# Attention and routed experts on one core: maxima, values and layer norms move from VectorE to ScalarE and GpSimd

## What is computed

```python
x = x + _layernorm(_L0_attn_ref(_layernorm(x), w_qkv, w_out, b_out))
x = x + _layernorm(_L0_ffn_ref(_layernorm(x), ...))
# _L0_ffn_ref:
for l in range(L):                                   # L = 2
    x = x + _attn(_ln(x, ln1_w[l], ln1_b[l]), wq[l], ..., bv[l], bo[l])
    h = _ln(x, ln2_w[l], ln2_b[l])
    moe = _token_moe if l % 2 == 0 else _seq_moe     # 2 of 8 experts, by token or by sequence
    x = x + moe(h, gate_w[l], gate_b[l], e_w1[l], e_b1[l], e_w2[l], e_b2[l])
# _attn: v = x @ wv + bv ; y = softmax(q k / sqrt(8), causal) @ v ; return y @ wo + bo
```

## Time and profile before

| | before |
|---|---|
| median of 3 runs | 1293.72 us (1292.19 to 1295.46) |
| the profiled execution | 1296.67 us |
| its span | 1295.0 us |
| TensorE busy | 1063.0 us (82%) |
| VectorE busy | 966.4 us (75%) |
| ScalarE busy | 711.1 us (55%) |
| GpSimd busy | 663.9 us (51%) |
| granted TensorE clock, mean | 0.957 |

### The profile page before, as it was taken

One profiled execution on the slowest core, in us unless ns is written; L12 is line 12 of the kernel. 1 busy time (PEld: TensorE's weight loads), 2 busy tenths in 40 slices (PEclk: granted clock), 3 DMA queues, 4 the chain that ended last, 5 costly groups with the idle time before them and its releaser, 6 DMA issues. The chain is left out here.

```text
span 1295.0 us, 36482 instructions
## 1 busy us (share of the span) xinstructions
PE 1063.0 (82%) x10163; PEld 786.2 (61%) x10258; DVE 966.4 (75%) x3059; ACT 711.1 (55%) x1502; POOL 663.9 (51%) x986
## 2 busy tenths in 40 slices
PE   1788888888899888888369999178788888868997
PEld 0565555556666565656269999145455555547996
DVE  3789999999989999899533333178888989855665
ACT  1466566666666656655145655145566566644564
POOL 3345555555555777776721111555666767422332
PEclk9999999999999999999679999589999999988999
DMA  5332111111111221121022222233312212100000
GB/s 148 99 92 68 50 49 34 41 49 51 52 45 40 63 65 49 54 62 43 33 87 70 72 69 70 66 104 101 86 42 64 63 40 62 51 2 5 20 19 22
DMA packets 120792, 74.56 MB, mean 58 GB/s; under 512 B 7936, under 2 KB 115712, under 8 KB 120704
## 3 DMA queue, kind: packets, MB, share of 16 engines
q1 hardware_dynamic: 101536, 54.48, 15.1%
q10 hardware_dynamic: 15072, 10.61, 2.9%
q0 software_dynamic: 4096, 8.40, 2.2%
HBM read 22.21 MB, written 12.71 MB: 27 GB/s over the span
## 5 line engine op out<-in xcount | busy, mean ns | idle before, releaser
L489 ACT ACTIVATE prob<-bank 128x512 f32<-128x512 f32 x576 | 341.5, 597 | 264.1 <-PE bank L319 151.5
L560 DVE TENSOR_REDUCE negm<-bank 128x2 f32<-128x512 f32 (+1 forms) x576 | 388.6, 678 | 53.0 <-PE bank L297 43.1
L861 POOL TENSOR_SCALAR_AFFINE_SELECT prob<-prob 128x512 f32<-128x512 f32 x384 | 248.7, 650 | 168.3 <-ACT prob L489 166.5
L338 PE MATMUL bank<-prob,vaug 128*32 128x256 f32 (+1 forms) x3072 | 165.9, 334 | 1.5 <-POOL prob L861 1.2
L305 PE MATMUL bank<-stack 126*128 126x256 bf16 x768 | 149.2, 275 | 0.0
L324 PE MATMUL bank<-stack 128*128 128x256 bf16 x768 | 147.8, 273 | 0.9 <-ACT prob L489 0.9
L1152 POOL COPY w_job<-w_s 128x512 f32 x72 | 47.1, 655 | 192.2 <-PE bank L1122 183.5
L1133 PEld LDWEIGHTS bank<-w_job,prob 128*128 128x128 f32 x1152 | 139.7, 192 | 3.6
L1133 PE MATMUL bank<-w_job,prob 128*128 128x128 f32 x1152 | 139.9, 275 | 0.0
L1144 ACT ACTIVATE prob<-bank,b_job 128x256 f32<-128x256 f32 x288 | 118.2, 469 | 16.1 <-PE bank L1122 14.6
L338 PEld LDWEIGHTS bank<-prob,vaug 128*32 128x32 f32 x3072 | 80.8, 109 | 75.7 <-issue 43.2
(11 more groups left out here) (174 smaller groups left out, 1971.6 us busy)
## 6 DMA issues: line engine op xcount, KB each, us to landing
stack<-parts SPq DMA_DIRECT2D x288, 128.0 KB
w_s<-e_w ACTq DMA_DIRECT2D x32, 256.0 KB, 2.9
oT<-x_routed SPq DMA_DIRECT2D x40, 128.0 KB, 2.1
y_routed<-oT SPq DMA_DIRECT2D x40, 128.0 KB, 1.8
stack<-mT SPq DMA_DIRECT2D x192, 4.0 KB
out<-x_all SPq DMA_DIRECT2D x16, 128.0 KB, 1.8
b_all<-e_b ACTq DMA_DIRECT2D x2, 512.0 KB, 8.3
x_routed<-hk,x_at POOLq DMA_INDIRECT x64, 2.3
```

What stands on the lines that cost most here:

```text
L338: m = nc.tensor.matmul(o, w, (prob0, prob1)[kb][:, g % 2, h], start=kb == 0, stop=kb == 1, skip_group_check=True)
L489: nc.scalar.activation(o, s, ACT.Exp, scale=SCALE).then_inc(exp_done, 1)
L560: nc.vector.tensor_reduce(o, s, AX.X, ALU.max, negate=True).then_inc(max_done, 1)
L861: nc.gpsimd.affine_select(out=t, in_=t, compare_op=ALU.is_ge, fill=0.0, base=0, pattern=[[0, HG], [1, P]], channel_multiplier=-1).then_inc ...
```

## The change

Eight things change, all of them in the attention pipelines:

- mT is copied by ScalarE (`act_mT`, after the slot's first exponential) instead of VectorE.
- v is copied to vaug by ScalarE without its bias (`act_values`, first in slot 3). The bias is folded into the output bias once at the start: since the softmax weights sum to one, bv @ wo is added to bo (`pe_fold_T`, `act_fold`, `pe_fold`, `dve_fold`).
- v's products go to slot 2 and to another bank (the upper half of `mid_bank`), behind a wait for mT; the waits on `v_sb` stand before transposes of maxima.
- xn is made by ScalarE (`act_xn`, slot 3, after mT) as Identity(r x + c), with c = -mean r made by GpSimd (`pool_shift`, two small operations after the root).
- hn likewise (`act_hn`, end of slot 2).
- f likewise (`act_f`, end of slot 1, where it was in slot 0 on VectorE).
- att of phase 0 is made by GpSimd (`pool_att`, last of its slot 2's own work); `dve_x` waits for it.
- Counters of the semaphores follow.

```diff
-        v_bank, lg_bank = post_bank[:, 0:T], post_bank[:, T:T + 2 * E]
+        v_bank, lg_bank = mid_bank[:, T:2 * T], post_bank[:, T:T + 2 * E]
         rank_bank, sum_bank = post_bank[:, T + 4 * E:T + 6 * E], post_bank[:, T + 6 * E:T + 7 * E]
+        fold_bank = [pv_bank[:, n * P:(n + 1) * P] for n in range(3)]
...
-            pe.wait_ge(res, NRES * i.v + NRES)
+            pe.wait_ge(hn_ok, 2 * (i.v - B) + 2)
...
-                if nxt:
-                    pe.wait_ge(v_sb, nxt.v + 1)
...
+                if gm == 0:
+                    pe.wait_ge(v_sb, im.v + 1)
+                if gm == 2 and nxt:
+                    pe.wait_ge(v_sb, nxt.v + 1)
                 pe_max_T(im, gm)
...
-            if k == 1 and nxt:
+            if k == 2 and nxt:
+                if im:
+                    pe.wait_ge(mT_sb, 4 * im.v + gm + 1)
                 pe_v(nxt)
...
+        def act_mT(i, g):
+            act.wait_ge(maxT_ps, 4 * i.v + g + 1)
+            need(act, row_dma[g % 2], rows_ready(i, g) - 16)
+            nc.scalar.copy(mT[:, g % 2], mid_bank[0:2 * HG, 0:P].bitcast(BF16)).then_inc(mT_sb, 1)
...
+        def act_values(i):
+
+            act.wait_ge(v_ps, i.v + 1)
+            need(act, pv_ps, 4 * (i.v - 2) + 4)
+            if isinstance(i.v, int) and i.v == 0:
+                act.wait_ge(kstack_ok, 2)
+            nc.scalar.copy(vaug[:, i.par].rearrange("p j h c -> p (j h) c")[:, :, 0:HD],
+                           v_bank.rearrange("p (s d) -> p s d", d=HD)).then_inc(v_sb, 1)
...
+        def pe_fold_T():
+
+            pe.wait_ge(later_ld, LATER)
+            for n in range(3):
+                m = nc.tensor.transpose(fold_bank[n], bv_s[:, n], ident[:])
+            m.then_inc(fold_ps, 1)
...
+        def pe_fold():
+            pe.wait_ge(fold_sb, 3)
+            for n in range(3):
+                m = nc.tensor.matmul(fold_bank[n], bvT[:, n], wo_s[:, n], start=True, stop=True)
+            m.then_inc(fold_ps, 1)
...
+        def dve_fold():
+            dve.wait_ge(fold_ps, 2)
+            for n in range(3):
+                nc.vector.tensor_tensor(bo_s[:, n], fold_bank[n], bo_s[:, n], ALU.add).then_inc(bo_ok, 1)
...
+        def act_normal(dst, src, r, c, s):
+
+            for j in range(2):
+                nc.scalar.activation(dst[j], src[j], ACT.Identity, scale=r[:, j:j + 1],
+                                     bias=c[:, j:j + 1]).then_inc(s, 1)
...
+        def act_xn(i):
+            act.wait_ge(pre_rstd, NPRSTD * i.v + NPRSTD)
...
+        def act_hn(i):
+            act.wait_ge(post_rstd, NRSTD * i.v + NRSTD)
+            need(act, hT_ps, i.v - B - 1)
+            if i.phase == 1:
+                need(act, hk_sb, i.v - B - 1)
+            act_normal([hn[:, i.par, j] for j in range(2)], tiles(f_all, i), post_r[:, i.par], post_c[:, i.par],
...
+        def act_f(i):
+            act.wait_ge(post_rstd, NRSTD * i.v + NRSTD)
+            act_normal(tiles(f_all, i), tiles(x_all, i), r2[:, i.par], c2[:, i.par], f_ok)
...
-            cur, nxt, nxt2, old, older = (item(step, d) for d in (0, 1, 2, -1, -2))
...
+            cur, nxt, nxt2, old, older, oldest = (item(step, d) for d in (0, 1, 2, -1, -2, -3))
...
+            if k == 3 and nxt:
+                act_values(nxt)
             if io:
                 act_oT(io, go)
             if ie:
                 act_exp(ie, ge, 0)
+            if im:
+                act_mT(im, gm)
+            if k == 3 and nxt2:
+                act_xn(nxt2)
...
+            if k == 1 and oldest and oldest.phase == 0:
+                act_f(oldest)
+            if k == 2 and older and older.phase > 0:
+                act_hn(older)
...
-        def dve_mT(i, g):
-            dve.wait_ge(maxT_ps, 4 * i.v + g + 1)
-            need(dve, row_dma[g % 2], rows_ready(i, g) - 16)
-            nc.vector.tensor_copy(mT[:, g % 2], mid_bank[0:2 * HG, 0:P].bitcast(BF16)).then_inc(mT_sb, 1)
...
+            need(dve, post_rstd, NRSTD * (i.v - 2) + 4)
+            dve_moments(post_st, post_mv[:, i.par], res, summed(i), 1 if i.phase == 0 else NRES - 5)
 
         def dve_x(i):
 
-            dve.wait_ge(res, NRES * i.v + 7)
+            dve.wait_ge(post_rstd, NRSTD * i.v + 4)
...
-                dve.wait_ge(res, NRES * (i.v - B) + NRES)
+                dve.wait_ge(f_ok, 2 * (i.v - B) + 2)
...
-            if im:
-                dve_mT(im, gm)
...
-            if k == 3 and nxt2:
-                dve.wait_ge(pre_rstd, 2 * nxt2.v + 2)
-                need(dve, xT_ps, nxt2.v - 1)
-                dve_normal([xn[:, nxt2.par, j] for j in range(2)], tiles(x_all if nxt2.phase == 0 else f_all, nxt2),
-                           pre_mv[:, nxt2.par], pre_r[:, nxt2.par], xn_ok)
...
-            if k == 0 and oldest and oldest.phase == 0:
-                dve_f(oldest)
...
-            if k == 2 and nxt:
-                dve_values(nxt)
...
-            if k == 2 and older:
-                dve_normalise(older)
...
+        def pool_shift(mv, r, c, s, base, last=1):
+
+            pool.wait_ge(s, base)
+            alone(pool)
+            for j in range(2):
+                nc.gpsimd.tensor_scalar(c[:, j:j + 1], mv[:, j, 0:1], r[:, j:j + 1], -1.0, ALU.mult,
+                                        ALU.mult).then_inc(s, last if j else 1)
+
+        def pool_att(i):
+            base = NRSTD * i.v + 2
+            pool.wait_ge(post_rstd, base)
+            alone(pool)
+            for j in range(2):
+                nc.gpsimd.tensor_scalar(att[:, i.par, j], att[:, i.par, j], post_mv[:, i.par, j, 0:1],
+                                        post_r[:, i.par, j:j + 1], ALU.subtract, ALU.mult).then_inc(post_rstd, 1)
...
-                pool_rstd(post_mv[:, older.par], post_r[:, older.par], post_rstd, NRSTD * older.v,
-                          1 if older.phase == 0 else NRSTD - 1)
+                if older.phase > 0:
+                    need(pool, hn_ok, 2 * (older.v - 2 - B) + 2)
+                pool_rstd(post_mv[:, older.par], post_r[:, older.par], post_rstd, NRSTD * older.v)
+                if older.phase > 0:
+                    pool_shift(post_mv[:, older.par], post_r[:, older.par], post_c[:, older.par], post_rstd,
+                               NRSTD * older.v + 2, NRSTD - 3)
             if k == 0 and oldest and oldest.phase == 0:
-                pool.wait_ge(res, NRES * oldest.v + 12)
-                pool_rstd(mv2[:, oldest.par], r2[:, oldest.par], post_rstd, NRSTD * oldest.v + 2)
+                pool.wait_ge(res, NRES * oldest.v + NRES)
+                need(pool, f_ok, 2 * oldest.v)
+                pool_rstd(mv2[:, oldest.par], r2[:, oldest.par], post_rstd, NRSTD * oldest.v + 4)
+                pool_shift(mv2[:, oldest.par], r2[:, oldest.par], c2[:, oldest.par], post_rstd,
+                           NRSTD * oldest.v + 6)
...
-                pool_rstd(pre_mv[:, nxt2.par], pre_r[:, nxt2.par], pre_rstd, 2 * nxt2.v)
+                pool_rstd(pre_mv[:, nxt2.par], pre_r[:, nxt2.par], pre_rstd, NPRSTD * nxt2.v)
+                pool_shift(pre_mv[:, nxt2.par], pre_r[:, nxt2.par], pre_c[:, nxt2.par], pre_rstd,
+                           NPRSTD * nxt2.v + 2)
...
+            if k == 2 and older and older.phase == 0:
+                pool_att(older)
...
+                act_fold()
...
-            run_steps(pe, behind(pe_slot, 0, [lambda: pe.wait_ge(later_ld, LATER)]), *RUNS[0])
+            run_steps(pe, behind(pe_slot, 0, [pe_fold_T, pe_fold, lambda: pe.wait_ge(bo_ok, 3)]), *RUNS[0])
```

70 lines of the change are left out of this document (29 added, 41 removed).

## The result

The changed kernel takes 1322.39 us (median; 1321.51 to 1324.33) against 1294.59 for the kernel before in the same comparison: a ratio of 1.022 (95% interval 1.020 to 1.0239). The forecast was 1267, its range 1238 to 1302; the time lies outside it, on the other side. The profiled execution took 1324.33 us with a span of 1322.6, so all that follows is read against a span that grew by 27.6 us.

A forecast was written before the change was run, and what follows sets the result against it. VectorE was taken as the nearest bound, TensorE close behind. TensorE waits saved, 55.6 us, less 18, 7 and 4 gave 26.6 off 1296.67: 1270, and 1267 with the median 3.0 lower; range 1238 to 1302.

The forecast's parts named there:

- Step (d): Stage zero's att on GpSimd: 0.6 us late for VectorE's x unless the chain moves up; taken as 0, bound 10 us.
- Rival 4: att on GpSimd is late and VectorE's x waits: 1267 + 10 = 1277 us; chance 0.47 together with the forecast.
- Step (b): Stages one and two: ScalarE stops in slot 2 for GpSimd's shift, making xT late: 0.25 a step, 7 us.
- rival 3: ScalarE's in-order queue stops for the shift, decided beyond 1.2 us behind slot 2's last exponential: 1328, likelier 1310; chance 0.19.
- The sign that was to refute the forecast: TensorE's waits for ScalarE (exponentials, mT, xT) coming to more than 25 us.
- Step (a): mT's copy ends later on ScalarE, delaying row transfer and next slot's scores: 0.4 us a step, 18 us.
- The wait for mparts: TensorE's wait for VectorE before the transposes of the maxima: half of 30.2 us to go, leaving near 15.
- The wait for `on`: TensorE's wait for VectorE before the attention output's transposes: 22.9 us to go, under 5 left.
- The products' waits: TensorE's waits for VectorE before three kinds of maximum products: 6.8, 6.7 and 4.1 us, all to go.
- its 11 us for hn: hn on ScalarE: 7 us for its queue stopping for the shift, 4 us at the ends of the two runs.
- The contention term: GpSimd's shift and att hold VectorE up through shared SBUF interfaces: would change the sum by under 5 us.
- Busy times: Profile after: VectorE near 810 us busy, ScalarE near 885, GpSimd near 720, TensorE unchanged at 1063.

The follow-up runs named there:

- att and hn back: Changed kernel with att and hn both normalised on VectorE again: 1275.2 us, ratio 0.9854 to the kernel before.
- att back: Changed kernel with only att of stage zero normalised on VectorE again: 1294.4 us, ratio 1.0007 to the kernel before.
- hn back: Changed kernel with only hn normalised on VectorE again, its GpSimd shift removed: 1305.6 us, ratio 1.0093 to the kernel before.
- fastest kernel: Changed kernel with att, hn and later stages' xn on VectorE, v products in slot 1, f_all addition behind the second reduction: 1259.2 us.

## Why the prediction was wrong

*The reading of the bound was right.* VectorE was what TensorE waited for, and relieving it pays: the same change without its worst moves is 2.0 to 2.7% faster. That the forecast's 2.1% lies there is luck, since its terms were off in both directions. "att and hn back" has a step of 16.8 in stage zero where 17.3 was forecast.

*Step (d), att on GpSimd, is the main error: taken at 0, bounded at 10 us, measured 28.* It failed twice. The price, 0.33 us, was put between a 128x2 operation and a 128x256 copy because the size lies between. The copy was no kin: it has no pointer scalars and, at twice the size, takes half the time of what was measured, 0.794. With 1.58 us for the pair in place of 0.7 the prediction's own working gives 212.3 instead of 211.5, 1.4 us late and some 23 us over 16 items. The second failure is the cover. "VectorE now has 3.9 us to make it up" treats spare load as if it could be spent in advance. VectorE's queue is in order, `on` and a reduction stand behind x, and TensorE needs both in the same slot: a stop of 2.76 us wasn't made up by being idle elsewhere. Rival 4 was the right mechanism with the wrong size.

The Trainium skill (GPSIMD Engine Reference, 4.1 Engine selection) gives elementwise work to VectorE and calls GpSimd's one-input operations roughly line-rate. The row bears out the first half and not the second: 794 ns on GpSimd against the 522 ns of att on VectorE.

*Step (b), hn on ScalarE: 7 us taken for the queue and 4 for the ends, 17 to 19 measured.* The wait was forecast at the right instruction, and the shift's end came 0.97 us behind the last exponential (511.69 against 510.72), short of rival 3's 1.2. But the working followed the delay only to xT at the end of slot 3, where 5.8 us of work give it time, and passed over oT, the second thing behind hn, which has none: TensorE's first transposes of slot 3 waited 21.0 us (28.3 with att back). Rival 3 ended on the right side by a mechanism next to the real one. The sign that was to refute the forecast, TensorE's waits for ScalarE above 25 us, has the same gap: it listed exponentials, mT and xT, which come to 6.3 us, and not oT with its 21.0.

*Step (a), the row transfer: 18 us against the change, and the wait fell by 26.* The copy is hardly later on ScalarE (2.1 us in all where mT is moved alone). And the v products, whose move the prediction took at nothing, are what fills the time before the row lands: with them back in slot 1 the wait is 35.8 to 39.2 us in four kernels. An edit costed at nothing was the one that moved the two largest waits of TensorE.

*The wait for mparts: half of 30.2 was to go, and it rose to 35.8.* The relief is real but small, 4.3 us where only mT is moved; the v products taken out of slot 1 opened the rest.

*The wait for `on`: under 5 us forecast, 27.8 measured,* 1.9 as soon as att is back. The products' waits were 17.6 before and 19.1 after (17.7 + 1.4); in stages one and two a stretched addition holds them, and moving it shifts most of that wait.

*What is left.* With att and hn back the kernel takes 1275.2 us, where the forecast without its 11 us for hn would be 1256. Of these 19 us no single part is the cause: in that kernel TensorE still waits 35.9 us for mparts and 19.5 for the maximum products, where 15.1 and nothing were forecast. The last steps of stage two, forecast at 18.7, stay at 20.0 with hn back and 19.9 with att and hn back; they are 19.2 with xn on VectorE as well, and 18.6 with the v products in slot 1 besides. How these share the loss of stage two stays open.

*The contention term,* "under 5 us", wasn't measured as a whole. Moving the stretched addition gave 0 in two comparisons and 4.3 us in the fastest kernel, where the two intervals overlap slightly, but other operations stay stretched.

*Busy times:* VectorE 870.6 where 810 was forecast. By groups, the removed operations are gone in full (162.8 us), but the addition to f_all grew by 13.1 us, the cast to mparts by 12.9 and x by 5.6, nearly all of them beside work on GpSimd. That is 31.6 of the 67 us by which the fall is short of 162.8; nearly all of the rest is overlap of records: VectorE's groups sum to 110 us more than its busy time before, and to 78 us more after. ScalarE shows 833.8 against 885: its records of back-to-back operations overlap.

## What to carry to other kernels

Where engines with in-order queues are coupled slot by slot, the relief of the busiest one counts for little against the first stop put into any queue. For each moved operation ask who stands behind it in the new queue, up to the next thing that another engine waits for at once, and price the stop there; spare load elsewhere does not pay for it. Move only those operations whose inputs are ready when the new queue reaches them: here the copies, f and stage zero's xn, and not att and hn, nor, as it seems, the later xn. Price an operation for a slower engine from a row of the same form, not from one of the same size. And count work that is moved between slots as a change, even if its amount stays: it is the filling of some wait.

## What the runs showed of the hardware

- GpSimd's elementwise operation with two pointer scalars, 128x128, takes 794 ns; a 128x256 copy takes 403, and the shift, 128x1 with one pointer scalar, 260 to 267 in the means of its three uses.
- GpSimd holds up VectorE's operations with two SBUF inputs. The addition of 128x256 takes 0.42 us alone and 1.89 us (1044.06 to 1045.95) where it lies beside the end of GpSimd's `y_got` (1043.49, 0.97 us) and its `rest` (1044.48, 1.17 us). The Trainium skill (GPSIMD Engine Reference, Key points) says that GpSimd and VectorE contend on such instructions; the trace agrees, with an addition that ends only after the GpSimd operations have. The cast to mparts, with one input, is stretched too: 0.17 us alone, up to 0.95 beside GpSimd's work.
- ScalarE starts an operation before the record of the one before it ends: 512.61, 512.86 and 513.12 are starts of operations recorded with 0.35, 0.37 and 0.60 us. The groups that the change added to ScalarE sum to 170 us, its busy time grew by 123.
- An Identity with two pointers on 128x128 is 483 to 489 ns on ScalarE in all its uses, as in the earlier trace rows (487; the prediction took its share of busy time, 0.44).
- TensorE's granted clock fell to its lower level for some 3 us after stretches in which it was busy 0.53 and 1.14 of 2 us, and 16 value products then took 1.51 us instead of 0.86. The mean clock of stage two was between 0.91 and 1.00 in kernels that differ by a few microseconds of waits in it.
